# A new table of steps for the projections of two 16-wide attentions

## The chip, the cores and the metric

The program runs on one core of a Trainium2 chip. The metric is the device time of one execution in microseconds. Three runs of the kernel before took 2673.93, 2677.01 and 2681.13 us; the median is 2677.01.

## What is computed

Sixteen sequences (`B`) of 112 positions (`S`) and 256 features pass through eight layers, four attentions over a context of 375 positions and four expert layers, each with a layer norm ahead and its result added to `x`. The change touches the first and the last attention, which have 16 heads of width 16:

```python
qh = heads(layernorm(x) @ Wq + bq);  kh = heads(ctx @ Wk + bk)
vh = heads(ctx)                      # first attention
vh = heads(ctx @ Wv + bv)            # last attention; scores masked by position
att = softmax(qh @ kh.T / sqrt(16), axis=-1)
x = x + merge(att @ vh) @ Wo + bo
```

## The kernel before

Both attentions are one function, `narrow_attention_phase` (L549), called as `a0` with `ctx` (values are the context itself) and as `a6` with `Wv`, `bv` and a mask. A layer norm phase goes ahead of each; its SyncE block already fetches weights, the context of two batches and constants.

Each engine has its own program, written out in an order that is a function of a step number `s`; semaphores tie the programs together. One step is one pair of heads of one batch: step `s` holds the score product of pair `s` (`score`, L919, 112 x 375 for two heads) and the *turned* scores of pair `s - 13` (`LAG` = 13; `score_turned`, L931: context positions by queries, with the negated maximum added in the product through two more rows of keys and queries). A batch is eight steps, so what belongs to batch `b` is placed by `t = s - 8b`, and below "step 0 to 7" is `t` modulo 8. VectorE takes the maximum of every score pair (`maximum`, L850), ScalarE the exponential of every turned pair (`exponentiate`, L786). In every odd step TensorE also multiplies two pairs with the values (`weigh`, L950), the *values product*. Scores and turned scores share three double banks in rotation.

All else TensorE does are *units*, given by `units_at(s)`: they all use the one PSUM bank `p`, so each waits until the one before it has been emptied (`emptied`), TensorE waiting in order. The units, who empties the bank, and where they stand before:

- `k` (two halves of the key projection of a batch, 6 matmuls each, L970; ScalarE L809 to `raw`, then GpSimd L749 and L751 split it into high and low parts): t = -13, -12, that is steps 3, 4
- `q` (two halves of the query projection of four batches, 4 fp32 matmuls each, L974; same way): t = -11, -10 of every fourth batch, steps 5, 6
- `v` (last attention only, L981, emptied by ScalarE L815): t = 5 (12 matmuls, two thirds) and 7 (6 matmuls)
- `m` (the split maxima turned, L988; ScalarE L821, then two DMAs L716 into the query rows): t = 10, step 2
- `turn_y` (L993; emptied by VectorE's reciprocal L865 and product `yn` L867): t = 22, step 6
- `turn_n` (L996; ScalarE L823): t = 24, step 0; `out` (L999; VectorE L873 adds to `X`): t = 25, step 1
- `w` (last attention only, once, at the first step: the bias of the values through `Wo`, added by VectorE L892)

Ahead of a key projection the context is loaded by SyncE (`load_context`, L630, t = -24), copied to fp16 by ScalarE (`high_context`, L793, t = -17) and its low part made by GpSimd (`split_context`, L755, t = -16). After it SyncE copies the split keys in six DMAs to their rows (`stack_keys`, L695; two more of the mask, L700, in the last attention; t = -11); the split queries likewise (`stack_queries`, L709, t = -9 of every fourth batch); `stack_maxima` is at t = 10, and `load_values` (L633, first attention) at t = -6. GpSimd also adds the output bias to `X` (L778) and copies the values (L773). VectorE splits a batch's maxima (L856, L858) at t = 8. Within a step each engine goes through its list in a fixed order: ScalarE first `high_context`, then `exponentiate`, then the emptying of the bank; GpSimd first the splits of units, then `split_context`; SyncE goes through the batches from the lowest up, so `stack_keys` of an older batch stands ahead of `load_context` of a newer one in the same step. Nothing passes anything else on its engine. Steps begin at `FIRST` = -14.

Of the kernel before, what the change touches and what calls it, by code (L numbers as in the profile page):

```python
# [14 lines left out]
B, S, D = 16, 112, 256  # L15
SK, KT, KP = 375, 3, 125
DC = D // 128
H = 16
# [530 lines left out]
def narrow_attention_phase(nc, tag, X, XT, ident, ctxT, Wq, Wk, Wo, bo, bq, bk, ctx=None, Wv=None, bv=None, mask=None):  # L549
# [8 lines left out]
    SLOTS = ((HI, HI), (LO, HI), (HI, LO))  # L558
    N_STACK = 2 * len(SLOTS) + (2 if mask is not None else 0)
    N_CONST = 2 * (2 if mask is not None else 1)  # L560
    FIRST, LAST = -14, 8 * (B - 1) + LAG + 12

    def units_at(s):

        found = [("w", 0, 0)] if s == FIRST and bv is not None else []
        for b in range(B):
            t = s - 8 * b
            found += [("k", b, t + 13)] if t in (-13, -12) else []
            found += [("q", b // GT, t + 11)] if t in (-11, -10) and b % GT == 0 else []
            found += [("v", b, (t - 5) // 2)] if t in (5, 7) and Wv is not None else []  # L570
            found += [("m", b, 0)] if t == 10 else []
            found += [("turn_y", b, 0)] if t == LAG + 9 else []
            found += [("turn_n", b, 0)] if t == LAG + 11 else []
            found += [("out", b, 0)] if t == LAG + 12 else []
        return found

    order = [unit for s in range(FIRST, LAST + 1) for unit in units_at(s)]
# [8 lines left out]
    with ExitStack() as st:  # L586
# [98 lines left out]
        with nc.Block() as block:  # L685
            @block.sync
            def _(sp):
                def stack_keys(b):
                    u = b % 4
                    sp.wait_ge(low_made, raw_number["k", b, 1] + 1)  # L690
                    if b >= 4:
                        sp.wait_ge(shifted, NP * (b - 3))
                    for r in range(2):
                        for i, (_, part) in enumerate(SLOTS):
                            sp.dma_start(k[64 * r + 16 * i:64 * r + 16 * i + 16, u, :, :],  # L695
                                         k_parts[:, b % 2, part, r, :]).then_inc(k_in[u], 16)
                        if mask is not None:
                            if b == 0 and r == 0:
                                sp.wait_ge(mask_made, 1)
                            sp.dma_start(k[64 * r + 48:64 * r + 50, u, :, :],  # L700
                                         mask_row[b:2 * B:B, :].unsqueeze(1).to_broadcast([2, NP, SK])).then_inc(k_in[u], 16)

                def stack_queries(g):
                    sp.wait_ge(low_made, raw_number["q", g, 1] + 1)
                    if g >= 2:
                        sp.wait_ge(shifted, NP * GT * (g - 1))
                    for r in range(2):
                        for i, (part, _) in enumerate(SLOTS):
                            sp.dma_start(q[64 * r + 16 * i:64 * r + 16 * i + 16, g % 2, :, :],  # L709
                                         q_parts[:, part, r, :]).then_inc(q_in[g % 2], 16)  # L710

                def stack_maxima(b):
                    g, t = divmod(b, GT)
                    sp.wait_ge(emptied, number["m", b, 0] + 1)
                    for r in range(2):
                        sp.dma_start(q[64 * r + KS:64 * r + KM, g % 2, :, t * S:(t + 1) * S],  # L716
                                     mT[16 * r:16 * r + 16, b % 2, :]).then_inc(m_in[b % 2], 16)

                for s in steps:
                    for b in range(B):  # L720
                        t = s - 8 * b
                        if t == -11:
                            stack_keys(b)
                        if t == -9 and b % GT == 0:
                            stack_queries(b // GT)
                        if t == -6 and ctx is not None and b >= 2:
                            sp.wait_ge(v_made, b - 1)
                            load_values(sp, b)
                        if t == -24 and b >= 2:
                            sp.wait_ge(kc_split, b - 1)  # L730
                            load_context(sp, b)
                        if t == 10:
                            stack_maxima(b)

            @block.gpsimd
            def _(pool):
# [24 lines left out]
                for s in steps:  # L761
# [2 lines left out]
                            split(unit)  # L764
                    for b in range(B):
                        t = s - 8 * b
                        if t == -16 and b >= 1:
                            split_context(b)
                        if t == 8 and ctx is not None:
                            pool.wait_ge(v_in[b % 2], 16 * (b // 2 + 1))  # L770
# [10 lines left out]
            def _(act):  # L781
# [7 lines left out]
                def high_context(b):  # L789
                    act.wait_ge(kc_in[b % 2], 16 * (b // 2 + 1))  # L790
                    if b >= 4:
                        act.wait_ge(projected, number["v" if Wv is not None else "k", b - 4, 1] + 1)
                    act.copy(kc16[:, b % 4, HI, :, :], kc[:, b % 2, :, :]).then_inc(kc_hi, 1)  # L793

                def take_y(b):
# [5 lines left out]
                def evacuate(unit):  # L801
# [7 lines left out]
                        act.activation(raw[:, n % 2, 0:width], p_bank[:, 0:width], ACT.Identity,  # L809
                                       bias=bias[:, c:c + 1], scale=by).then_inc(emptied, 1)  # L810
                    elif kind == "v":
                        blocks = (2, 1)[c]
                        if b >= 2:
                            act.wait_ge(weighed, 4 * (b - 1))
                        act.mul(values[:, b % 2, 2 * c:2 * c + blocks, :, 0:HD],  # L815
                                p_bank[0:KP, 0:blocks * D].rearrange("p (j h d) -> p j h d", h=H, d=HD),
                                1.0 / WS).then_inc(emptied, 1)
                    elif kind == "m":
                        if b >= 2:
                            act.wait_ge(m_in[b % 2], 32 * (b // 2))  # L820
                        act.copy(mT[:, b % 2, :], p_bank[0:32, 0:S]).then_inc(emptied, 1)  # L821
                    else:
                        act.copy(yT[:, :, :], p_bank[:, 0:DC * S].rearrange("p (c s) -> p c s", s=S)).then_inc(emptied, 1)  # L823
# [7 lines left out]
                act.wait_ge(ones_made, 1)  # L831
                for s in steps:
                    for b in range(1, B):
                        if s == 8 * b - 17:
                            high_context(b)
                    p = s - LAG
                    if 0 <= p < NPAIR:
# [8 lines left out]
            def _(dve):  # L846
# [36 lines left out]
                for s in steps:  # L883
                    if 0 <= s < NPAIR:
                        maximum(s)
                    for b in range(B):
                        if s == 8 * b + 8:
                            split_maxima(b)
                    for kind, b, _ in units_at(s):
                        if kind == "w":  # L890
# [9 lines left out]
            def _(pe):  # L900
# [35 lines left out]
                def weigh(n):  # L936
# [4 lines left out]
                    if blk == 0:  # L941
                        if ctx is not None:
                            pe.wait_ge(v_made, b + 1)
                        else:
                            pe.wait_ge(emptied, number["v", b, 1] + 1)
                        if b >= 1:
                            pe.wait_ge(y_out, b)
                    for j in range(KT):
# [7 lines left out]
                def project(unit):  # L956
# [18 lines left out]
                                           start=i == 0, stop=i == DC - 1)  # L975
                    elif kind == "v":
                        pe.wait_ge(w_split, 2)
                        for j in ((0, 1), (2,))[c]:
                            for n, (x, z) in enumerate(PARTS):
                                for i in range(DC):  # L980
                                    mm = pe.matmul(p_bank[0:KP, (j % 2) * D:(j % 2 + 1) * D],  # L981
                                                   kc16[:, b % 4, x, i, j * KP:(j + 1) * KP], wv16[:, z, i, :],
                                                   start=n == i == 0, stop=(n, i) == (2, DC - 1))
                    elif kind == "m":
                        pe.wait_ge(split_done, b + 1)
                        if b == 0:
# [1745 lines left out]
```

## Time and profile before

| | us |
|---|---|
| median of 3 runs | 2677.01 |
| profiled execution | 2686.12 |
| its span | 2684.2 |
| TensorE busy in the span | 2262.7 (84%) |
| VectorE, ScalarE, GpSimd busy | 1483.1, 1281.2, 954.4 |

The profiled execution is one run; its span goes from the first to the last instruction, and the rest of its time lies around it. "Busy" is time in which an instruction of the engine runs. Times in the rows are microseconds from the span's start. PEclk is the granted clock of TensorE as a share of full speed (1.00 is 2.4 GHz, 0.50 is 1.2 GHz). The name behind `<-` in square brackets is what ended the idle time before an instruction. The name before `<-` in an instruction is the tile it writes, those behind it the ones it reads. A DMA's duration on SyncE is that of its issue; when its data has landed is told by the DMA view.

### The profile page before, as it was taken

What the parts mean: (1) busy time and instruction counts of PE and PEld (TensorE: products, weight loads), DVE (VectorE), ACT (ScalarE), POOL (GpSimd) and SP (SyncE); (2) the same over time, 40 slices, a digit from 0 to 9 for tenths busy, and PEclk for the clock granted to TensorE, in tenths of its full rate; (3) what the DMA queues carried; (4) which work ended last, traced back from release to release, by engine and by line L of the source; (5) the groups of instructions that cost most, each with busy time, mean ns of one, the idle gap of its engine ahead of it and who ended that gap; (6) DMA issues with size and microseconds to landing.
All of it is one profiled execution on the core that took longest, in us unless ns stands there. A gap on an engine that the chain in (4) does not pass through costs nothing. (4 is left out here: it accounts for less than half of the span.)

```text
span 2684.2 us, 60296 instructions
## 1 busy us (share of the span) xinstructions
PE 2262.7 (84%) x23000; PEld 1484.9 (55%) x23000; DVE 1483.1 (55%) x3516; ACT 1281.2 (48%) x2643; POOL 954.4 (36%) x1066
## 2 busy tenths in 40 slices
PE   4898589689999999858599999999974993899746
PEld 2555345367777777636356666666652541566523
DVE  3666482476666656456655555555555544555463
ACT  2555463265555555434355445445453542555543
POOL 3443132154445444313323233233323732333043
PEclk7898689899999999969799999999987995999868
DMA  5553271310000000010200000000023215333033
GB/s 112 107 111 81 76 235 37 106 31 14 14 14 8 14 14 2 2 32 1 90 8 13 8 13 14 8 13 8 1 79 98 68 59 121 75 76 72 19 113 109
DMA packets 118570, 139.43 MB, mean 52 GB/s; under 512 B 15072, under 2 KB 107184, under 8 KB 118288
## 3 DMA queue, kind: packets, MB, share of 16 engines
q1 hardware_dynamic: 110900, 115.39, 16.6%
q0 software_dynamic: 7392, 20.19, 2.4%
q8 instruction: 192, 3.15, 0.5%
q14 instruction: 86, 0.70, 0.1%
HBM read 93.25 MB, written 17.47 MB: 41 GB/s over the span
## 5 line engine op out<-in xcount | busy, mean ns | idle before, releaser
L850 DVE TENSOR_REDUCE a_mx<-a_pair 112x2 f32<-112x750 f32 x256 | 234.4, 934 | 203.7 <-PE a_pair L919 203.6
L302 POOL TENSOR_SCALAR a_P<-a_P,a_inv 112x375 f32<-112x375 f32 x256 | 148.4, 593 | 454.8 <-DVE a_inv L412 454.8
L1160 POOL TENSOR_TENSOR a_kp<-a_kp 125x512 f16<-125x512 f32 x192 | 217.6, 1158 | 259.2 <-ACT a_kp L1251 259.2
L786 ACT ACTIVATE a_PT<-a_pair 125x672 f32<-125x672 f32 x256 | 186.4, 731 | 101.1 <-PE a_pair L931 99.4
L340 ACT ACTIVATE a_P<-a_masked,a_least 112x375 f32<-112x375 f32 x256 | 153.5, 601 | 100.6 <-DVE a_least L407 100.6
L407 DVE CUSTOM_DVE_ANT_0 a_masked<-a_s,a_mask_add 112x375 f32<-112x375 f32 x256 | 129.6, 544 | 59.5 <-PE a_s L507 59.5
L427 DVE SCALAR_TENSOR_TENSOR a_k<-a_p,a_k 128x375 f16<-128x375 f32 x128 | 70.4, 550 | 152.9 <-ACT a_k L351 152.9
L474 PE MATMUL a_p<-a_kc,a_wk 128*128 128x375 f16 x768 | 147.0, 327 | 4.9 <-POOL a_kc L296 4.1
L1251 ACT CAST a_kp<-a_kp 125x512 f16<-125x512 f32 x192 | 110.4, 617 | 76.3 <-DVE a_kp L1313 76.3
L1393 PE MATMUL a_p<-a_kc,a_wk 128*128 128x375 f16 x768 | 142.2, 326 | 5.4 <-POOL a_kc L1152 5.4
L1294 DVE SCALAR_TENSOR_TENSOR a_k<-a_p,a_k 128x375 f16<-128x375 f32 x128 | 69.3, 547 | 139.0 <-ACT a_k L1207 138.9
L488 PE MATMUL a_p<-a_wv,a_kc 128*125 128x512 f16 x576 | 142.4, 383 | 2.6 <-DVE a_k L427 2.5
L1393 PE MATMUL a_p<-a_wv,a_kc 128*125 128x512 f16 x576 | 141.0, 385 | 0.0
L2322 PE MATMUL f_hb<-w_w1h,f_x 128*128 x588 | 136.1, 370 | 0.0
L2406 ACT ACTIVATE all_XT<-f_hb 128x512 f32<-128x512 f32 (+1 forms) x98 | 53.2, 549 | 160.1 <-PE f_hb L2322 124.2
L1313 DVE TENSOR_SCALAR a_kp<-a_p 125x512 f32<-125x512 f32 x192 | 122.7, 680 | 8.2 <-PE a_p L1424 8.2
L351 ACT ACTIVATE a_k<-a_p 128x375 f16<-128x375 f32 x128 | 61.8, 483 | 124.7 <-PE a_p L474 124.7
L517 PE MATMUL a_t<-all_ident,a_P 112*125 112x112 f32 x768 | 116.3, 287 | 0.3 <-POOL a_P L302 0.3
L419 DVE COPY a_PT<-a_t 125x336 f32<-125x336 f32 x256 | 115.4, 492 | 1.2 <-PE a_t L517 1.1
L931 PE MATMUL a_pair<-a_q,a_k 50*125 50x112 f16 (+1 forms) x1536 | 93.2, 229 | 25.6 <-DVE a_mx L850 17.5
L517 PEld LDWEIGHTS a_t<-all_ident,a_P 112*125 112x125 f32 x768 | 93.4, 188 | 36.0 <-issue 34.9
L970 PE MATMUL a_p<-a_kc,a_wk 128*128 128x375 f16 x384 | 89.5, 379 | 25.9 <-POOL a_kc L755 10.8
(415 smaller groups left out, 5170.4 us busy)
## 6 DMA issues: line engine op xcount, KB each, us to landing
a_kc<-in_ctxT SPq DMA_DIRECT2D x64, 375.0 KB, 3.6
a_k<-a_k_parts SPq DMA_DIRECT2D x192, 93.8 KB
w_stage<-in_L_ffn_W SPq DMA_DIRECT2D x32, 512.0 KB
w_stage<-in_L_ffn_ew SPq DMA_DIRECT2D x16, 512.0 KB, 7.0
w_stage<-expert_rows SPq DMA_DIRECT2D x16, 448.0 KB, 7.5
a_v_in_sb<-in_ctx SPq DMA_DIRECT2D x16, 375.0 KB
a_q<-a_q_parts SPq DMA_DIRECT2D x48, 112.0 KB, 3.6
w_stage<-in_L_ffn_W SPq DMA_DIRECT2D x16, 256.0 KB, 4.0
```

The costliest lines, as they stand in the source:

```text
L302: pool.tensor_scalar(P[:, p % 4, r, :], P[:, p % 4, r, :], inv[:, p % 4, r:r + 1], 1.0, ALU.mult, ALU.mult).then_inc(P_done, 1)
L340: act.activation(P[:, p % 4, r, :], masked[:, p % 2, r, :], ACT.Exp, bias=least[:, p % 4, r:r + 1], scale=-1.0, accum_out=total[:, p % 4, ...
L407: dve.tensor_tensor_reduce(masked[:, p % 2, r, :], s_bank[0:S, r, 0:SK], mask_add[:, b % 2, :], 1.0, 3e38, ALU.add, ALU.min, least[:, p % ...
L474: mm = pe.matmul(out[:, 0:SK], wk16[:, z, j, c * 128:(c + 1) * 128], kc16[:, b % 2, x, j, :], start=i == j == 0, stop=(i, j) == (2, DC - 1))
L488: mm = pe.matmul(out[0:KP, 0:512], kc16[:, b % 2, x, j, jk * KP:(jk + 1) * KP], wv16[:, z, j, w * 512:(w + 1) * 512], start=i == j == 0, s ...
L517: mm = pe.transpose(t_bank[0:KP, r, j * S:(j + 1) * S], P[:, p % 4, r, j * KP:(j + 1) * KP], ident[0:S, 0:S])
L786: act.activation(PT[:, p % 4, :, :], pair_bank[slot["turned", p]][0:KP, :, 0:KT * S], ACT.Exp).then_inc(exp_done, 1)
L850: dve.tensor_reduce(mx[:, b % 2, 2 * pair:2 * pair + 2], pair_bank[slot["score", p]][0:S, :, 0:SK], AX.X, ALU.max).then_inc(max_done, 1)
L1160: pool.tensor_tensor(kp16[:, LO, j, hf, r, :, :].rearrange("p c m -> p (c m)"), kp[:, n % 4, :], kp16[:, HI, j, hf, r, :, :].rearrange("p ...
L1313: dve.tensor_scalar(kp[:, n % 4, :], p_bank[bank][0:KP, 0:512], 0.0, EPS * WS, ALU.max, ALU.add).then_inc(f_evac, 1)
L1393: mm = pe.matmul(out, lhs(x, z, j), rhs(x, z, j), start=i == j == 0, stop=(i, j) == (2, DC - 1))
L2322: mm = pe.matmul(bank[:, 0:BW], x16[:, j % 2, x, c, :], w.w1h[:, z, c, bass.ds(e, 1), cols].rearrange("p o f -> p (o f)"), start=False, st ...
```

## The change

`units_at` reads its places from named constants, some of which are new:

- `k` at t = -16 and -12 (steps 0 and 4) instead of -13 and -12
- `q` at t = -29 and -21 of every fourth batch (both step 3, eight steps apart) instead of -11 and -10; stack_queries at -13 instead of -9
- `v` as three units of 6 matmuls at t = 5, 6, 7 instead of two of 12 and 6
- `m` at t = 9 instead of 10, VectorE's split of the maxima at 7 instead of 8
- `turn_n` at t = 25 instead of 24, `out` at 26 instead of 25
- `load_context` at t = -27 instead of -24, `high_context` at -21 instead of -17, `split_context` at -19 instead of -16
- steps begin at -29, so the first group's order is q, q, k, k instead of k, k, q, q; the last step is one later

Where two units fall in one step, the one of the older batch goes first: `turn_n` ahead of `m` in step 1, `turn_y` ahead of `v` in step 6. The amounts of work are unchanged.

```diff
--- before.py
+++ after.py
@@ -558,20 +558,22 @@
     SLOTS = ((HI, HI), (LO, HI), (HI, LO))
     N_STACK = 2 * len(SLOTS) + (2 if mask is not None else 0)
     N_CONST = 2 * (2 if mask is not None else 1)
-    FIRST, LAST = -14, 8 * (B - 1) + LAG + 12
+    FIRST, LAST = -29, 8 * (B - 1) + LAG + 13
+    K_AT, Q_AT, V_AT, M_AT = (-16, -12), (-29, -21), (5, 6, 7), 9
+    TURN_Y, TURN_N, OUT = LAG + 9, LAG + 12, LAG + 13
 
     def units_at(s):
 
         found = [("w", 0, 0)] if s == FIRST and bv is not None else []
         for b in range(B):
             t = s - 8 * b
-            found += [("k", b, t + 13)] if t in (-13, -12) else []
-            found += [("q", b // GT, t + 11)] if t in (-11, -10) and b % GT == 0 else []
-            found += [("v", b, (t - 5) // 2)] if t in (5, 7) and Wv is not None else []
-            found += [("m", b, 0)] if t == 10 else []
-            found += [("turn_y", b, 0)] if t == LAG + 9 else []
-            found += [("turn_n", b, 0)] if t == LAG + 11 else []
-            found += [("out", b, 0)] if t == LAG + 12 else []
+            found += [("k", b, K_AT.index(t))] if t in K_AT else []
+            found += [("q", b // GT, Q_AT.index(t))] if t in Q_AT and b % GT == 0 else []
+            found += [("v", b, V_AT.index(t))] if t in V_AT and Wv is not None else []
+            found += [("m", b, 0)] if t == M_AT else []
+            found += [("turn_y", b, 0)] if t == TURN_Y else []
+            found += [("turn_n", b, 0)] if t == TURN_N else []
+            found += [("out", b, 0)] if t == OUT else []
         return found
 
     order = [unit for s in range(FIRST, LAST + 1) for unit in units_at(s)]
@@ -721,12 +723,12 @@
                         t = s - 8 * b
                         if t == -11:
                             stack_keys(b)
-                        if t == -9 and b % GT == 0:
+                        if t == -13 and b % GT == 0:
                             stack_queries(b // GT)
                         if t == -6 and ctx is not None and b >= 2:
                             sp.wait_ge(v_made, b - 1)
                             load_values(sp, b)
-                        if t == -24 and b >= 2:
+                        if t == -27 and b >= 2:
                             sp.wait_ge(kc_split, b - 1)
                             load_context(sp, b)
                         if t == 10:
@@ -764,7 +766,7 @@
                             split(unit)
                     for b in range(B):
                         t = s - 8 * b
-                        if t == -16 and b >= 1:
+                        if t == -19 and b >= 1:
                             split_context(b)
                         if t == 8 and ctx is not None:
                             pool.wait_ge(v_in[b % 2], 16 * (b // 2 + 1))
@@ -789,7 +791,7 @@
                 def high_context(b):
                     act.wait_ge(kc_in[b % 2], 16 * (b // 2 + 1))
                     if b >= 4:
-                        act.wait_ge(projected, number["v" if Wv is not None else "k", b - 4, 1] + 1)
+                        act.wait_ge(projected, number[("v", b - 4, 2) if Wv is not None else ("k", b - 4, 1)] + 1)
                     act.copy(kc16[:, b % 4, HI, :, :], kc[:, b % 2, :, :]).then_inc(kc_hi, 1)
 
                 def take_y(b):
@@ -809,11 +811,9 @@
                         act.activation(raw[:, n % 2, 0:width], p_bank[:, 0:width], ACT.Identity,
                                        bias=bias[:, c:c + 1], scale=by).then_inc(emptied, 1)
                     elif kind == "v":
-                        blocks = (2, 1)[c]
                         if b >= 2:
                             act.wait_ge(weighed, 4 * (b - 1))
-                        act.mul(values[:, b % 2, 2 * c:2 * c + blocks, :, 0:HD],
-                                p_bank[0:KP, 0:blocks * D].rearrange("p (j h d) -> p j h d", h=H, d=HD),
+                        act.mul(values[:, b % 2, c, :, 0:HD], p_bank[0:KP, 0:D].rearrange("p (h d) -> p h d", d=HD),
                                 1.0 / WS).then_inc(emptied, 1)
                     elif kind == "m":
                         if b >= 2:
@@ -831,7 +831,7 @@
                 act.wait_ge(ones_made, 1)
                 for s in steps:
                     for b in range(1, B):
-                        if s == 8 * b - 17:
+                        if s == 8 * b - 21:
                             high_context(b)
                     p = s - LAG
                     if 0 <= p < NPAIR:
@@ -884,7 +884,7 @@
                     if 0 <= s < NPAIR:
                         maximum(s)
                     for b in range(B):
-                        if s == 8 * b + 8:
+                        if s == 8 * b + 7:
                             split_maxima(b)
                     for kind, b, _ in units_at(s):
                         if kind == "w":
@@ -942,7 +942,7 @@
                         if ctx is not None:
                             pe.wait_ge(v_made, b + 1)
                         else:
-                            pe.wait_ge(emptied, number["v", b, 1] + 1)
+                            pe.wait_ge(emptied, number["v", b, 2] + 1)
                         if b >= 1:
                             pe.wait_ge(y_out, b)
                     for j in range(KT):
@@ -975,12 +975,10 @@
                                            start=i == 0, stop=i == DC - 1)
                     elif kind == "v":
                         pe.wait_ge(w_split, 2)
-                        for j in ((0, 1), (2,))[c]:
-                            for n, (x, z) in enumerate(PARTS):
-                                for i in range(DC):
-                                    mm = pe.matmul(p_bank[0:KP, (j % 2) * D:(j % 2 + 1) * D],
-                                                   kc16[:, b % 4, x, i, j * KP:(j + 1) * KP], wv16[:, z, i, :],
-                                                   start=n == i == 0, stop=(n, i) == (2, DC - 1))
+                        for n, (x, z) in enumerate(PARTS):
+                            for i in range(DC):
+                                mm = pe.matmul(p_bank[0:KP, 0:D], kc16[:, b % 4, x, i, c * KP:(c + 1) * KP], wv16[:, z, i, :],
+                                               start=n == i == 0, stop=(n, i) == (2, DC - 1))
                     elif kind == "m":
                         pe.wait_ge(split_done, b + 1)
                         if b == 0:
```

## Rows read from the trace of the kernel before

**Rows 1.** Windows: stretch, length, busy time (instructions) by engine, clock, DMA share, GB/s
```profile
51.65:108.42 56.77, 46.04 (x468) 24.80 (x469) 33.86 (x43) 25.40 (x41) 26.35 (x33) 0.76 0.57 103
108.42:246.60 138.18, 124.57 (x1850) 78.30 (x1846) 90.43 (x131) 83.45 (x144) 64.03 (x79) 0.99 0.53 107
164.34:176.89 12.55, 11.58 (x187) 7.51 (x183) 8.54 (x14) 8.15 (x15) 5.81 (x8) 1.00 0.53 109
2273.32:2333.80 60.48, 52.34 (x541) 31.48 (x541) 32.38 (x43) 28.91 (x48) 24.02 (x29) 0.84 0.39 84
2333.80:2491.95 158.15, 145.34 (x2029) 97.19 (x2028) 87.54 (x130) 93.55 (x163) 57.44 (x71) 1.00 0.32 71
2398.30:2413.03 14.73, 13.76 (x202) 9.44 (x201) 8.50 (x13) 9.15 (x16) 5.06 (x7) 1.00 0.25 67
```

**Rows 2.** Timeline, TensorE, plain batch, first attention: start, duration (us), line, shapes, [idle <-releaser]
```profile
166.09 0.78 PE L950 MATMUL a_y<-a_PT,a_values 125*32 125x112 f32 x24
166.80 1.12 PE L999 MATMUL a_p<-a_wo,a_yT 128*112 128x256 f32 x4
167.85 0.37 PE L919 MATMUL a_pair<-a_k,a_q 48*112 48x375 f16 x2
...
170.31 1.14 PE L970 MATMUL a_p<-a_kc,a_wk 128*128 128x375 f16 x6
...
171.37 0.37 PE L919 MATMUL a_pair<-a_k,a_q 48*112 48x375 f16 x2
...
172.11 1.14 PE L970 MATMUL a_p<-a_kc,a_wk 128*128 128x375 f16 x6 [0.20 <-ACT a_raw L809]
```

**Rows 3.** Timeline, TensorE, second query product of a pair, first attention
```profile
147.49 1.77 PE L974 MATMUL a_p<-all_XT,a_wq 128*128 128x448 f32 x4 [0.81 <-DVE a_yn L867]
```

**Rows 4.** Timelines of ScalarE, GpSimd, SyncE; DMA view (us to landing) of two loads
```profile
173.28 0.57 ACT L809 ACTIVATE a_raw<-a_p,a_bkT 128x375 f32<-128x375 f32 x1 [0.60 <-PE a_p L970]
...
173.76 0.73 ACT L786 ACTIVATE a_PT<-a_pair 125x672 f32<-125x672 f32 x1
...
175.63 0.81 ACT L793 CAST a_kc<-a_kc 128x750 f16<-128x750 f32 x1
...
173.92 0.50 POOL L749 CAST a_k_parts<-a_raw 128x375 f16<-128x375 f32 x1 [0.26 <-ACT a_raw L809]
174.50 0.90 POOL L751 TENSOR_TENSOR a_k_parts<-a_raw,a_k_parts 128x375 f16<-128x375 f32 x1
...
162.87 3.80 SPq L695 DMA_DIRECT2D a_k<-a_k_parts  x6
...
a_kc<-in_ctxT SPq DMA_DIRECT2D x1, 375.0 KB, 4.1
...
a_kc<-in_ctxT SPq DMA_DIRECT2D x1, 375.0 KB, 5.2
```

**Rows 5.** Timeline, TensorE, values projections of a batch, last attention
```profile
2408.27 1.52 PE L981 MATMUL a_p<-a_wv,a_kc 128*125 128x256 f16 x12
...
2412.23 0.87 PE L981 MATMUL a_p<-a_wv,a_kc 128*125 128x256 f16 x6
```

**Rows 6.** Timelines of TensorE and ScalarE, starts of both attentions
```profile
34.33 3.36 PE L974 MATMUL a_p<-all_XT,a_wq 128*128 128x448 f32 x4 [0.66 <-ACT a_raw L809]
...
52.48 0.82 ACT L793 CAST a_kc<-a_kc 128x750 f16<-128x750 f32 x1 [1.70 <-DMA a_kc<-in_ctxT]
...
2273.32 1.19 PE L919 MATMUL a_pair<-a_k,a_q 50*112 50x375 f16 x6 [1.94 <-DMA a_q<-a_q_parts]
...
2276.77 2.04 PE L970 MATMUL a_p<-a_kc,a_wk 128*128 128x375 f16 x6 [1.30 <-POOL a_kc L755]
```

**Rows 7.** Timelines of VectorE (two splits of maxima) and GpSimd, first attention
```profile
151.83 2.82 DVE L858 SCALAR_TENSOR_TENSOR a_m<-a_mx,a_m 112x16 f16<-112x16 f32 x1
...
165.93 0.18 DVE L858 SCALAR_TENSOR_TENSOR a_m<-a_mx,a_m 112x16 f16<-112x16 f32 x1
...
153.11 1.51 POOL L755 TENSOR_TENSOR a_kc<-a_kc 128x750 f16<-128x750 f32 x1
```

## Prediction

> **What bounds the kernel now.** The change touches one function, which runs twice: the first attention (scores start at 51.65 us) and the last one (2273.32). I first measured, with the windows view, the stretch from one score product to another. A batch of 112 queries is eight steps, one pair of heads each. In the middle of the first attention a batch without a query projection takes 12.55 us, in which TensorE is busy for 11.58, VectorE for 8.54, ScalarE for 8.15 and GpSimd for 5.81, at full clock (1.00, the 2.4 GHz level); in the last attention it is 14.73, with TensorE at 13.76 [rows 1]. So TensorE's own sequence sets the step, and what can be won is only its holes. Ten batches in the middle take 138.18 and 158.15 us; ten plain ones would be 125.5 and 147.3, so each of the two pairs of query projections among them costs (138.18 - 125.5) / 2 = 6.3 and 5.4 us. The first four batches take 56.77 and 60.48 us, at a mean clock of 0.76 and 0.84: there the 1.2 GHz level and the hand-overs count.
>
> The holes are read in the TensorE timeline. A values product (weigh) and what stands before the next unit takes 166.80 - 166.09 = 0.71 us; the output product 1.05; a key projection 171.37 - 170.31 = 1.06, the second of the pair starting 0.2 late because the single bank `p` is still being emptied by ScalarE [rows 2]. A score and its turned scores take 0.47 without a wait (estimate from the same starts). Plain sum: 8 x 0.47 + 4 x 0.71, the two key products, output 1.05, turns and maxima about 1.3: some 11.1, so 1.4 of 12.55 us is waiting: mostly a turned score behind VectorE's maximum after a step shorter than 1.2 us, the early second key product, and the y copy. For queries: 1.77 us each at full clock, and the second waits 0.81 more for `a_yn`, since it follows turn_y in one step [rows 3].
>
> **The change, part by part (first attention, plain batch).** I walk the new order through with these durations, step 0 starting at 0. Step 0: turned score still behind the last maximum of the batch before (0.54), then key product 0: 1.9. Step 1: score, turned, values product 1.18, turn_n 0.34, then the maxima's product, which now stands right behind turn_n in the same bank and waits for ScalarE's copy (0.5 estimate): 2.2. Step 2 gets the output product: 1.55. Step 3 loses its key product: 1.18. Step 4: 1.6, its wait on the bank gone. Steps 5, 6, 7 as before: 1.18, 1.45, 1.18. Sum 12.26, so at most 0.3 us a batch. Splitting maxima one step sooner costs VectorE the same two short operations; the maxima's DMAs start as much sooner as the steps between got shorter, and are needed 2.8 us later, as now.
>
> The queries stand alone in step 3 of two different batches: 1.77 plus 0.25 because step 4's key product then waits for the bank: 2.0 each, 4.0 a pair.
>
> **The moved context.** high_context goes from t=-17 to -21 and its load from -24 to -27. But SyncE issues in order, and at t=-27 the load stands behind stack_keys of an older batch, which waits for GpSimd's split of a key product of the step before; so far it was sent right behind these too. The load thus leaves no sooner, while ScalarE wants it four steps sooner, in front of an exp. That closes a ring: copy 0.81, two exps 2 x 0.73, evacuation 0.57, GpSimd 0.50 + 0.90, six key issues 3.80, landing 4.1 (5.2 at another batch) [rows 4]; with some 0.4 for hand-overs 12.5 us, or 13.6 with the later landing. It is as long as the batch. I take 12.65 for a batch without a query product, near the shorter landing, to which most are close. A batch with one has room: 12.26 + 2.0 = 14.3. The batch after the queries' stacking has 6 more DMAs ahead of keys and context: its context lands later by an estimated 1.3 us, near the 1.1 between the two landings (bounds 0 and 2.2). Four batches: 14.3 + 14.3 + 12.35 (room from before) + 13.6 = 54.5; ten: 2 x 54.5 + 2 x 12.65 = 134.3 against 138.18: **-3.9** (ring never binding, no backlog: 10 x 12.26 + 8.0 = 130.6, -7.6; ring at 13.6: 4 x 14.3 + 6 x 13.6 = 138.8, +0.6).
>
> **The last attention** has no load of values (ring shorter than the batch) but values projections. Now 12 matmuls in step 5 (1.52 us as drawn) and 6 in step 7 (0.87) [rows 5], each 0.07 less to the next start, as the key product in [rows 2]; after, 6 in each of steps 5, 6, 7: 2.4, that is +0.15. The one in step 6 stands behind turn_y in the same bank, and waits for the reciprocal and `yn` on VectorE, as the second query product does now (0.81) [rows 3]. In exchange the short steps are filled, and waits behind maxima go, 0.7. Walked through as above: 1.62 + 2.18 + 1.52 + 1.18 + 1.63 + 1.98 + 2.91 + 1.98 = 15.0, +0.3. Ten batches: 150.0 + 2 x 4.0 = 158.0 against 158.15: **-0.2** (no wait in step 6: -4; half a microsecond more a batch: +3). The two last batches add 0.3 each: **+0.5**, with the last units one step later at no cost, as no product is left in between.
>
> **The starts** are where I expect the loss. Query products come first: 3.36 us each at half clock [rows 6]. In the first attention they can start 3 us before the first key product could, so, by these durations in a row, the first score comes at about 47.7 instead of 51.65 (this time and those that follow are estimates of the same kind). But then: SyncE loads context 2 only behind stack_keys(0) (about 44.7, landing at 49); ScalarE at s=-5 waits for it *before* it evacuates the second key product of batch 1 (s=-4); GpSimd splits that one (1.4) and only then the context (1.6); and the key product that needs it stands at s=0 right behind the first score. It starts at about 53.5, and TensorE idles for 5 us. Then come the query product for the next group (3.36 + 0.6) and its evacuation behind the wait for context 3 (1.4). Score 8 is then at +3.8, score 16 at +6.1 (+4.9 if the clock has risen, +7.3 if not), and the 6.3 of the query pair is gone from batches 2 and 3: **-0.2** (-2.9 to +1.8).
> In the last attention the head start doesn't exist: the bias product `w` holds the bank until VectorE has added it, so queries start where keys did. First score +1.7 (eight key DMAs now come last); key product of batch 2 at 2280.2 instead of 2276.77 [rows 6], another +1.8; query product at half clock +4.0; ScalarE's wait for context 3 +1.8; one hand-over more among the values units +0.6: +9.9 at score 8. The other query product adds 2.5 (0.7 at full clock, 4.3 at half), and 5.4 comes back in batch 2: **+7.0** (+5.2 to +10).
>
> **Sum.** -0.2 - 3.9 + 7.0 - 0.2 + 0.5 = **+3.2 us**. The profiled execution took 2686.12 us (span 2684.2 and 1.9 around it), 9.1 above the median 2677.01 of three runs; the difference applies to both: 2689.3 profiled, **2680** as a median. A measurement of this kernel can tell about 0.3%, 8 us, from no change.
>
> **VectorE against GpSimd.** In a batch after a query pair a maxima split (L858) takes 2.82 us and ends with GpSimd's context split, which began after it and took 1.51; the same operation takes 0.18 where it isn't met [rows 7]. It delays the maxima behind it by 2.6 us. In the new order the context split (step 5) ends about 0.7 us before the maxima split begins, and the key split comes 2 us after it; that gain is in the 6.3 above.
> The Trainium skill (SBUF — State Buffer, "Who interferes with whom") says that a VectorE instruction with two SBUF inputs contends with a GpSimd instruction that reads SBUF, and that the first takes the shared pair for a whole instruction while the other fully blocks. The row doesn't agree in size: the wait of 2.6 is longer than any one GpSimd instruction there. The sum stays by either, as it is taken from the measured 138.18; the collision rival below would cost 1.2 us a batch by the rule and 2.3 by the row.
>
> **Rivals.**
> - *Slower: the context ring and chain.* For it: one landing of 5.2 us, the copy already waiting on it at the first batches [rows 4, 6], and a load that does not leave sooner. Against: most landings near 4.1. It decides from a landing of about 4.6 us on. Price: middle +0.6 instead of -3.9, first start +3.8, last start +10, the rest +0.3: +14.7, **2692**.
> - *Faster: the clock.* The starts miss 24% of full clock over 57 us and 16% over 60: 13.6 + 9.7 = 23 us where TensorE is the bound [rows 1]. If the longer unbroken stretches of query products win half of that back, the starts give +6.8 - 11.7 = -4.9, and all together -4.9 - 3.9 - 0.2 + 0.5 = -8.5: **2668**. Against: the 5 us hole in front of batch 2's keys.
> - *The split still collides.* If the later context copy makes GpSimd late by over 0.7 us, L858 blocks until that one instruction ends (1.5), in every batch, and with it step 1's turned score, which has 0.3 to spare: 1.2 x 10 on top of 3.2: +15, **2692**.
> - *The moved units do nothing for the middle*, because each wait comes back at another hand-over (ring at 12.55): +3, inside the forecast.
>
> **Chances.** Forecast (with the last rival) 0.47, faster by the clock 0.25, ring 0.19, collision 0.09. Faster by over 0.3%: 0.26; within: 0.47; slower: 0.27. Of the forecast's own bounds, 2672 to 2688. Range over the cases: **2665 to 2692**.
>
> **What would show it.** Plain batches of the first attention at 12.3 to 12.8 us, with ScalarE's idle time before the context copy released by the DMA; query pairs at 4 instead of 6.3; L858 at 0.18 everywhere; in the last attention, 15.0 a batch, with the second values unit waiting on `a_yn`; TensorE idle for about 5 us after the first scores, then waiting on `a_kc` from GpSimd. The prediction is wrong if score 32 of the last attention doesn't come later than 60.48 us after its first, if the context copy never waits on its DMA, or if the clock in the starts rises above 0.9.

## The result and the profile after

The changed kernel is **slower by 0.46%**: 2688.58 us median (2684.38 to 2694.59, 11 runs) against 2676.66 (2669.36 to 2681.13, 11 runs), ratio 1.0046 with a 95% interval of 1.0038 to 1.0054: +12 us, where +3 was forecast. It lies within the range (2665 to 2692), just above the forecast's own bounds (2672 to 2688), and in the class "slower by over 0.3%", which had a chance of 0.27. The first lines of its page:

```profile
span 2686.7 us, 60342 instructions
PE 2241.7 (83%) x23000; PEld 1480.5 (55%) x23000; DVE 1477.8 (55%) x3516; ACT 1294.0 (48%) x2659; POOL 956.6 (36%) x1066
```

The spans differ by 2.5 us only. That agreement with the sum is chance: the last expert layer, in which no line differs, takes 138.42 us in the profile before and 124.53 in this one (last section). The answer to [rows 1] is the windows view of the same stretches, from score 0 to score 32 and on to score 112, in both attentions, with single batches between them:

```profile
48.54:116.60 68.06, 46.74 (x467) 25.98 (x467) 32.24 (x45) 26.43 (x42) 27.08 (x32) 0.70 0.51 90
116.60:264.15 147.55, 125.39 (x1852) 81.81 (x1848) 86.42 (x129) 85.86 (x143) 63.99 (x80) 0.93 0.54 98
207.30:219.44 12.14, 11.32 (x188) 7.53 (x185) 8.69 (x14) 8.29 (x15) 5.71 (x8) 1.00 0.82 138
219.44:240.14 20.70, 13.23 (x189) 8.89 (x185) 8.96 (x14) 8.40 (x15) 5.91 (x8) 0.84 0.59 93
2288.39:2353.80 65.41, 52.08 (x539) 32.50 (x539) 32.52 (x45) 30.89 (x53) 24.77 (x29) 0.83 0.41 78
2353.80:2510.37 156.57, 142.60 (x2027) 96.81 (x2026) 87.84 (x130) 99.02 (x173) 57.53 (x71) 1.00 0.35 72
2402.28:2417.17 14.89, 13.60 (x203) 9.41 (x201) 8.78 (x13) 9.67 (x17) 5.05 (x6) 1.00 0.41 64
```

Its columns are those of [rows 1]. Third and fourth line are two neighbouring batches of the first attention, 10 and 11. A plain one now takes 12.14 (12.55 before), and the next 20.70, with the same work. Batches 3, 7 and 11 take 21.98, 20.84 and 20.69; the others of the middle 11.9 to 15.3. These are the batches that follow the stacking of a group's queries. ScalarE's waits in 116.60 to 264.15 (us in all, times, longest):

```profile
ACT a_kc L795 <- DMA a_kc<-in_ctxT: 24.4, 7, 8.4
ACT a_PT L788 <- PE a_pair L931: 19.6, 35, 1.3
```

The longest of the first kind, in the timeline (start, duration, and in brackets the idle time ahead of it), and the issue of the load that it waits for:

```profile
221.88 0.59 SPq L632 DMA_DIRECT2D a_kc<-in_ctxT  x1
...
233.29 0.82 ACT L795 CAST a_kc<-a_kc 128x750 f16<-128x750 f32 x1 [8.44 <-DMA a_kc<-in_ctxT]
```

The load was issued at 221.88, behind six key DMAs, which stand behind six query DMAs and a values load. It landed some 11.3 us later (an estimate: the copy that waits for it starts 11.4 after the issue), not 4.1 to 5.2 as in [rows 4]. TensorE stops, and afterwards the granted clock is 0.56, near the 1.2 GHz level, where 1.00 stood before. The windows view of batch 11:

```profile
221.50:225.50 4.00, 3.56 (x55) 2.47 (x53) 2.22 (x3) 2.49 (x5) 2.85 (x4) 1.00 1.15 123
225.50:227.30 1.80, 1.80 (x40) 1.23 (x37) 1.59 (x3) 0.00 (x0) 0.00 (x0) 1.00 0.91 146
227.30:233.30 6.00, 0.63 (x4) 0.18 (x2) 0.28 (x1) 0.01 (x1) 0.00 (x0) 0.93 0.35 84
233.30:240.14 6.84, 5.35 (x78) 4.00 (x78) 3.18 (x5) 5.01 (x8) 2.98 (x3) 0.56 0.22 63
```

In the six dead microseconds the DMA engines are at a mean share of 0.35 and 84 GB/s, though work is waiting. That would fit a last part of the backlog that lies on some of the engines only; the view doesn't name them, so this isn't shown.

### The profile page after: what moved, and what is told of

It is laid out like the page before. It is cut to its first block and busy times, and to the rows that moved or that the text cites. A ratio compares the mean times of both kernels' runs of the same rounds, so it can differ in the third digit from the quotient of the medians.

```text
span 2686.7 us, 60342 instructions
## 1 busy us (share of the span) xinstructions
PE 2241.7 (83%) x23000; PEld 1480.5 (55%) x23000; DVE 1477.8 (55%) x3516; ACT 1294.0 (48%) x2659; POOL 956.6 (36%) x1066
## 5 line engine op out<-in xcount | busy, mean ns | idle before, releaser
L340 ACT ACTIVATE a_P<-a_masked,a_least 112x375 f32<-112x375 f32 x256 | 153.5, 601 | 100.7 <-DVE a_least L407 100.7
L919 PE MATMUL a_pair<-a_k,a_q 48*112 48x375 f16 (+1 forms) x512 | 98.1, 386 | 28.0 <-ACT a_PT L788 21.5
```

The source lines that it names most:

```text
L340: act.activation(P[:, p % 4, r, :], masked[:, p % 2, r, :], ACT.Exp, bias=least[:, p % 4, r:r + 1], scale=-1.0, accum_out=total[:, p % 4, ...
```

## The experiments

Each job timed the kernel before on the same chip; its median was 2676.6 for e1 to e4 and 2689.5 to 2689.8 for e5 to e12, so only ratios are compared. The letters in the expectations are explanations: A (and A'), the query DMAs delay the context; B, the loss is in the last attention; C, the context copy stands too early; E, stacking and values load together ask more of the DMA engines than a batch allows; F, a stall follows every stacking.

**Which attention.** e1 has the new table in the first attention only, e2 in the last only. They choose it by a flag, `NEW = Wv is None` in one and `Wv is not None` in the other:

```diff
-    FIRST, LAST = -29, 8 * (B - 1) + LAG + 13
+    FIRST, LAST = (-29, 8 * (B - 1) + LAG + 13) if NEW else (-14, 8 * (B - 1) + LAG + 12)
...
+    STACK_Q, LOAD, COPY, SPLIT, MAXIMA = (-13, -27, -21, -19, 7) if NEW else (-9, -24, -17, -16, 8)
```

> The new table in the first attention only, the old one in the last. Theory A (the loss is the query stacking DMAs of t=-13, which hold up the context in the first attention, three times): the full kernel was 12 us above before; the first attention's phase grew by 12 us in the profiles, the last one's by 3. So about +9 to +12 us against before, with the 8 us steps at step 4 of batches 3, 7 and 11. Rival B (the loss sits in the last attention's start and values units): +2 us or less.

> The new table in the last attention only. Theory A: +1 to +4 us against before: start +6, middle -1.6, an end that is shorter. Rival B: +9 or more.

e1: 1.0058 (1.0041 to 1.0075), that is +15.5 us; e2: 1.0004 (0.9995 to 1.0013). So the loss is in the first attention; in the last one it is at most the +3.5 us of the interval's end. The profiles of the same job say it too: from the first attention's layer norm to the next phase 304.90 in e1 and 288.54 in e4 (the kernel before), and the last attention's phase 318.90 in e2 and 319.30 in e4. My main loss, the last attention's start, does not show in the time. By attention the forecast was -4.1 and +7.3 us, and the runs have +15.5 and +1.1.

**Queries stacked later.**

```diff
-                        if t == -13 and b % GT == 0:
+                        if t == -9 and b % GT == 0:
```

> The changed kernel with one number back: the queries are stacked at t=-9 (step 7, after the keys and the context load of step 5 have been issued) instead of -13 (step 3, right behind the values load). Theory A: the waits of ScalarE's context copy on its DMA fall from 8 us to about 1, step 4 of batches 3, 7, 11 from 8 to 9 us to about 1.7, the three batches from 21 to 13 or 14 us: 20 us less than the changed kernel, about 8 us below before. Rival C (the context copy at t=-21 is too early whatever stands in the queue; the ring of 12.5 us binds): less than 8 us is won back and the batches stay above 16 us.

1.0044 (1.0027 to 1.0060): nothing won, the expectation missed. The middle of the first attention is 140.88 instead of 147.55, but the last attention's rises to 162.35. Batch 7 still takes 18.23. TensorE now waits for the maxima, whose DMAs stand behind the queries, and ScalarE still for the context. From the waits views of ScalarE and of TensorE, 107 to 249 us:

```profile
ACT a_kc L795 <- DMA a_kc<-in_ctxT: 13.8, 7, 3.7
PE a_pair L931 <- DMA a_q<-a_mT: 7.4, 3, 3.0
```

**The kernel before again.**

> The kernel before, unchanged, for a second profile. The profiled execution shown was 9 us above the median of its runs, and its last phase (the last expert layer, 138.4 us) is 13.9 us longer than in the changed kernel, where no line of it differs. If that was chance of one execution, this profile has it at 124 to 130 us and a span near 2675; if the changed kernel really shortens it, it is 138 again.

Its last expert layer took 123.69 us: the 138.42 shown before is not the old kernel's. Its other stretches repeat [rows 1] within 0.3, but for the last attention's start, 63.55 instead of 60.48, and that phase as a whole, 319.30 instead of 312.76.

**The context copied later.**

```diff
-                        if s == 8 * b - 21:
+                        if s == 8 * b - 18:
...
-                        if t == -19 and b >= 1:
+                        if t == -17 and b >= 1:
```

> The changed kernel with the context copy at t=-18 (step 6) and its low part at -17 (step 7) instead of -21 and -19; loads and all else as changed. Theory C (the early copy turns late landings into stalls, whatever delays them): the load that now takes 11.3 us to land, because six query DMAs, a values load and six key DMAs are ahead of it, is wanted 4.6 us later, so ScalarE's wait of 8.4 us falls to some 4; batches 3, 7, 11 of the first attention go from 21 to about 16.5 us: 13 us less than the changed kernel. Both starts gain 2 to 3 us each, since the copy for batch 2 no longer stands ahead of batch 1's second key product: 2669 to 2674. Rival A (only the amount of DMA ahead matters): no more than 4 us less than the changed kernel.

1.0007 (0.9996 to 1.0019): by the ratios 10 us less than the changed kernel, but not where expected. The ten middle batches, where 13 us were to be won, give 3.3 (144.21 against 147.55). The copy waits for no DMA any more in the middle, yet batches 7 and 11 still take 17.52 and 20.82: the stall moved to the next thing that the same queue delivers. From TensorE's waits, 48.56 to 254.82:

```profile
PE a_pair L931 <- DMA a_q<-a_mT: 18.5, 3, 7.9
```

The starts did gain, 6 us in the first attention (68.06 to 62.05) and 7 in the last (65.41 to 58.35). The last attention's start takes 64.9 to 65.6 us in six profiles with the new table and the early copy (the changed kernel and e2, e6, e8, e9, e10), and 56.8 to 58.5 in the four with the late copy (e5, e7, e11, e12). The windows view of e5, the first attention's ten batches and the last one's start:

```profile
110.61:254.82 144.21, 125.38 (x1850) 81.60 (x1846) 86.33 (x129) 86.33 (x143) 64.33 (x80) 0.94 0.52 97
2276.15:2334.50 58.35, 48.19 (x539) 30.05 (x540) 32.50 (x45) 30.32 (x52) 23.57 (x27) 0.90 0.47 85
```

So theory C (the early copy makes the stall) falls for the middle, with the queue in this order, and holds for the starts.

**The burst in halves**, alone and with the late copy:

```diff
-                    for r in range(2):
+                    for r in sides:
...
-                            stack_queries(b // GT)
+                            stack_queries(b // GT, (0, 1) if b == 0 else (0,))
+                        if t == -5 and b % GT == 0 and b > 0:
+                            stack_queries(b // GT, (1,))
```

> The changed kernel with the burst of query DMAs parted: three of six at t=-13, the other three eight steps later at t=-5 (first group as before). Theory A' (the burst of DMAs ahead of keys and context is what makes the load late): landing falls from 11.3 to about 7 us, the waits of the copy from 8.4 to 3 or 4, now in two batches of four; the sum over a group falls by 3 to 6 us, 9 to 15 us less in all than the changed kernel. Theory C alone: 5 us less or nothing, as the wait is only spread.

> Both edits together. If early copy and burst are the two factors, no wait of the copy on its DMA is left in the middle batches: 12.2 us plain, 13.7 to 14 with a query product, four batches 52 to 53 us where the changed kernel has 69 and the kernel before 56 to 57; middle of the first attention 130 to 132 us against 147.5; the starts as in the kernel with the late copy. 2658 to 2666 in all, clearly below the kernel before.

1.0037 (1.0021 to 1.0054) and 1.0024 (1.0012 to 1.0035). Halves bring batches 7 and 11 from 21 to 18.8; three query DMAs suffice for a stall here. Together with the late copy it is worse than the late copy alone, a clear miss: the second half comes too late for the scores (waits of 11.2 us in three), and the maxima are late too (11.6 in three).

**What the backlog is made of.** The values load moved (`t == -2` instead of -6), left out, and the stackings of groups 2 and 3 left out. In e9 and e10 the waits that counted on what is gone are shortened to match; both leave out work that the result needs, so they serve for reading the traces alone:

```diff
-                        if t == -6 and ctx is not None and b >= 2:
+                        if False:
...
-                        if t == -13 and b % GT == 0:
+                        if t == -13 and b % GT == 0 and (ctx is None or b < 2 * GT):
```

> The changed kernel with the values load of the first attention at t=-2 (step 6, after keys and context of step 5) instead of -6 (step 2, just ahead of the queries). If the 375 KB of the values are a full part of the backlog: landing of the context after a query stacking 8 to 9 us instead of 11.3, batches 3, 7, 11 at 18 to 19 us instead of 21. If only the query DMAs count, they stay at 20 to 22.

> The changed kernel without the loads of the values of batches 2 to 15 in the first attention (the values of batches 0 and 1 are used again, so that part of the result is left out). Theory E (in the first attention the batch that holds the stacking of queries asks more of the DMA engines than its 12.2 us allow; in the last attention, which has no values load and 14.9 us a batch, the same stacking causes no wait): without 375 KB a batch, batches 3, 7, 11 fall from 21 to 12.5 to 14 us. If the six query DMAs alone did it, they stay above 18.

> The changed kernel without the query stacking of groups 2 and 3 in the first attention (the projections are still made and split; the old rows are used, so the scores of batches 8 to 15 are not the reference's). Theory E and theory A alike: batches 7 and 11 fall from 21 to 12.2 us, batch 3 stays at 21 to 23; the landing of the context there is 4 to 5 us. If they stay long, the queries' DMAs are not what delays the context.

e8: batches 3, 7, 11 fall to 12.93, 12.73, 12.14, and the batches ahead of them rise to 18.41, 20.13, 20.17, TensorE waiting for maxima (14.0 us in three): moved again. e9: batch 7 takes 14.37 and batch 11 13.44. e10: 12.96 and 13.05, while batch 3, whose stacking was left in, stays at 22.04. The ten batches and batch 7 of e9, in the windows view:

```profile
107.42:240.56 133.14, 121.21 (x1850) 78.93 (x1847) 87.03 (x131) 85.38 (x144) 64.09 (x81) 0.99 0.46 82
147.91:162.28 14.37, 12.52 (x188) 8.27 (x185) 9.53 (x16) 8.31 (x15) 5.91 (x8) 0.91 0.41 82
```

The same of e10:

```profile
114.37:246.78 132.41, 121.07 (x1850) 78.52 (x1846) 86.21 (x129) 85.17 (x143) 63.89 (x80) 0.99 0.48 99
155.52:168.48 12.96, 11.38 (x188) 7.57 (x184) 8.69 (x14) 8.18 (x15) 5.71 (x8) 1.00 0.56 107
```

Either load alone costs 0.8 to 2.2 us above a plain batch; both together, in this order and in a batch of 12 us, cost 8.6 to 9.8. That the stall needs both is shown by taking away each of them. That the length of the batch matters is argued: in the last attention the same six query DMAs, without a values load and in 14.9 us a batch, cause no such stall (14.89 for batch 7), but there both differ.

**The query products put beside the stacking.** The late copy is in both attentions. In the first one the query products also move, and the queries are stacked after the keys and the context load:

```diff
+    if Wv is None:
+        FIRST, Q_AT, STACK_Q, COPY, SPLIT = -19, (-13, -9), -8, -18, -17
```

> As the kernel with the late copy in both attentions, and in the first one the two query products are put into the batch whose stacking follows (t=-13 and -9, steps 3 and 7 of batches 2, 6, 10), stacked at t=-8. Theory E (the DMA engines need some 30 us for the two batches around a stacking, whatever TensorE does, so the products should be spent there): batches 2 and 3 of a group stay at 30 to 31 us together, batches 0 and 1 fall from 13.9 to 12.15: a group 54.5 to 55.5 us where the changed kernel has 61 to 62 and the kernel before 55.9 to 57.2; against the kernel before 8 to 12 us less. Rival F (a stall of 6 to 8 us follows a stacking, whatever is beside it): a group stays at 58 to 61 us.

0.9983 (0.9972 to 0.9994): 4 us under the kernel before, not 8 to 12. Batches 0 and 1 of a group fall to 12.14, but the two around the stacking take 15.77 and 18.25, 34.0 and not 30: a group 58.3, which is what rival F asked for. It isn't rival F's stall, though. From score 32 to score 112 no engine waits for a DMA. What holds up batch 7 is read in the timelines of TensorE, GpSimd and SyncE:

```profile
153.56 1.12 PE L977 MATMUL a_p<-a_kc,a_wk 128*128 128x375 f16 x6 [3.56 <-POOL a_kc L762]
...
150.27 0.56 POOL L756 CAST a_q_parts<-a_raw 128x448 f16<-128x448 f32 x1 [4.24 <-ACT a_raw L816]
150.91 1.03 POOL L758 TENSOR_TENSOR a_q_parts<-a_raw,a_q_parts 128x448 f16<-128x448 f32 x1
151.90 1.51 POOL L762 TENSOR_TENSOR a_kc<-a_kc 128x750 f16<-128x750 f32 x1
...
151.97 3.77 SPq L716 DMA_DIRECT2D a_q<-a_q_parts  x6
```

TensorE wants the low part of the context in step 0. GpSimd makes it only behind the split of the second query product, which e12 put into step 7, just ahead of it. The wait begins before the first query DMA is issued, and it stands in all three such batches (10.7 us together). The rest of the 6 us is the clock, 0.81 over the batch. So e12 shows a new wait on GpSimd, and no stall of the queue at all. Whether 30 us would be enough for the DMA engines (theory E) stays open, and a context split ahead of the query split was not tried.

**A version that beats both.**

> The old table in the first attention; the new one in the last, with the context copy at t=-18 and its low part at -17 there. The phase of the last attention was 308 us with this copy, 315 to 319 with the changed kernel's and 313 to 319 before: so 5 to 9 us below the kernel before, the only version so far that is faster than both. If the gain of the copy lies in the first attention alone, no difference from the kernel before.

The old table in the first attention, the new one with the late copy in the last: **0.9968 (0.9957 to 0.9979)**, 8 us under the kernel before, the lowest of all versions; e12 is the only other one below it. Its windows (first attention's ten batches, last one's start and ten batches) are the old ones in the first attention and e5's in the last:

```profile
106.68:245.34 138.66, 124.69 (x1852) 78.52 (x1848) 90.70 (x131) 83.43 (x144) 64.08 (x79) 0.99 0.54 106
2267.82:2326.35 58.53, 48.28 (x539) 30.16 (x540) 32.53 (x45) 30.28 (x52) 23.54 (x27) 0.90 0.47 85
2326.35:2482.92 156.57, 142.59 (x2027) 96.81 (x2026) 87.84 (x130) 98.02 (x173) 57.80 (x71) 1.00 0.36 72
```

## Why the prediction was right, and where it was not

The time lies in the range and on the side that was forecast, but this is luck in part. The forecast put the whole loss into the last attention and a gain into the first; e1 and e2 show it the other way round. The walk through the steps and the starts' mechanism held, one step failed badly, and an error of the other sign hid part of it. By stretches of the profiles (starts counted from the layer norm's first instruction, 11.13 and 2233.04 before, 11.27 and 2246.61 after), in us:

| term | forecast | measured |
|---|---|---|
| first attention, to score 32 | -0.2 | +8.0 |
| first attention, ten batches | -3.9 | +9.4 |
| last attention, to score 32 | +7.0 | +6.4 |
| last attention, ten batches | -0.2 | -1.6 |
| last batches and ends, both | +0.5 | -7.3 |
| both phases | +3.2 | +14.9 |

The rest of the span gave -12.4, of it -13.9 in the last expert layer; with +14.9 that is the 2.5 between the spans. Single profiles are a weak measure of two of the terms:

- The last attention to score 32, counted like this, took 100.7 and 106.2 us in the two profiles of the kernel before and 102.1 in e1, which has the old table there, so its +6.4 may be as little as +1.0. The changed kernel's last attention phase (315.53) is 2.8 longer than that of the profile before (312.76) and 3.8 shorter than e4's.
- The -7.3 of the ends is for the most part the clock of this one execution. From score 112 of the first attention to the next phase the changed kernel took 48.34 us at a mean granted clock of 0.91; e1 and e10, with the same table there, took 55.61 at 0.71; the kernel before 53.60 at 0.76. The windows view, changed kernel and then e1:

```profile
264.14:312.48 48.34, 36.16 (x619) 24.36 (x615) 20.49 (x36) 25.34 (x43) 3.67 (x5) 0.91 0.08 22
260.67:316.28 55.61, 45.05 (x619) 30.33 (x615) 20.76 (x38) 25.53 (x43) 3.67 (x5) 0.71 0.07 19
```

What held and what failed:

- **The failed step** is "its context lands later by an estimated 1.3 us (bounds 0 and 2.2)". The batch after a stacking took 20.7 to 22.0 us, 8.6 to 9.8 above the plain 12.14, three times: 27 us where I had some 4. The load landed 7 us later than in a plain batch, not 1.3. I took the bound from the spread of two landings that stood in no such queue. What I should have asked is what is issued ahead of the context load within one batch, before and after, and how soon the copy wants it. In the kernel before, too, the load stood right behind the six query DMAs, but the values load came after it, the keys had gone out 4 us earlier, and the copy asked for it only at 163.07 (L793) and didn't wait:

```profile
144.61 3.80 SPq L695 DMA_DIRECT2D a_k<-a_k_parts  x6
151.70 3.90 SPq L709 DMA_DIRECT2D a_q<-a_q_parts  x6
155.65 0.60 SPq L630 DMA_DIRECT2D a_kc<-in_ctxT  x1
156.85 1.35 SPq L716 DMA_DIRECT2D a_q<-a_mT  x2
158.25 0.42 SPq L633 DMA_DIRECT2D a_v_in_sb<-in_ctx  x1
```

- **The ring of 12.5 to 13.6 us** did not bind: plain batches took 12.14, where the sum had 12.65 and the walk 12.26, though the copy's short waits on the DMA (1.1 to 2.2 us) are there. Its danger was named in the right place and priced wrong, as a steady half microsecond and not as a stall of 8 us. The measured time is nearer to this rival's 2692 than to the forecast's 2680, but not by its mechanism.
- **The walk through the steps held.** Plain batches 12.14 (12.26 forecast) and 14.89 (15.0); a query pair in the last attention 3.9 (16.82 twice against 14.89) where 4.0 was forecast; the values unit behind turn_y waits 0.8 for `a_yn`.
- **The starts held in their mechanism**, though for the last attention e2's time doesn't show the loss: first score at 48.54 (47.7), the key product of batch 2 at 53.92 (53.5), after a hole of 4.81 that GpSimd's split ends:

```profile
53.92 2.04 PE L970 MATMUL a_p<-a_kc,a_wk 128*128 128x375 f16 x6 [4.81 <-POOL a_kc L757]
```

  The +8.0 of the first attention's start is the stall of batch 3; with a plain 12.14 there the start would be at -1.8. That the early copy costs 6 to 7 us in the starts is shown by e5, and by e11 in the last attention. The upper bound of +10 for the last start doesn't follow from its own terms (9.9 + 4.3 - 5.4 = 8.8).
- **VectorE against GpSimd**: L858 takes at most 176 ns in the whole changed kernel, so [rows 7] are gone, as said; the collision rival did not come. The 2.82 us of the kernel before lie beside three GpSimd instructions back to back (151.63 to 154.62 us), so the rule of the Trainium skill (SBUF — State Buffer, "Who interferes with whom") may have acted once for each; no run here measures a single collision.
- The clock rival fell: 0.70 and 0.83 in the starts, where 0.76 and 0.84 stood.

## What to carry to other kernels

When the order of transfers or the length of a batch changes, write down what is issued ahead of each load in one period, and when its reader wants it. Six query DMAs and a values load, both ahead of the keys and the context load, cost 8.6 to 9.8 us in a batch of 12.1; in the kernel before, with the values load behind and a later copy, the batch after the stacking was 1.4 us above a plain one (13.97 against 12.55).

A stall that moves from one waiting instruction to another when one of them is relaxed (context copy, maxima, scores, in e3, e5, e7 and e8) belongs to what they share, here the queue. But name the wait anew each time: the 18.25 us of e12 look like the same stall and are a wait for GpSimd.

A sum that fits the profile is not confirmed while phases outside the change differ, or while a term that fits does so by the clock of one execution.

## What the runs showed of the hardware

- The last expert layer took 122.9 to 127.7 us in five profiles (the changed kernel and e1 to e4 among them) and 136.4 to 141.9 in nine others, those of e5 to e12 and the first one of the kernel before; its code and TensorE time are much the same. In e1 to e12 the two kinds go with the jobs, not with the kernels, and so does the median of the kernel before (2676.6 with the short kind, 2689.5 to 2689.8 with the long one); why is open. The windows view of that layer in the changed kernel:

```profile
2562.14:2686.67 124.53, 67.42 (x505) 41.45 (x505) 74.67 (x243) 50.00 (x119) 54.32 (x55) 0.73 0.41 124
```

And in e11:

```profile
2534.70:2672.90 138.20, 70.67 (x505) 41.71 (x505) 74.93 (x243) 49.34 (x119) 53.90 (x55) 0.73 0.39 111
```

- A context load of 375 KB landed 4.2 us after its issue in plain batches and 11.3 after a stacking, with a mean DMA share of 0.35 in the last 6 us. Why the share is so low while a load is waited for is open; another queue for the queries was not tried.
- In the end of the first attention the same instructions took 48.3 us at a mean granted clock of 0.91 and 55.6 at 0.71 in different executions (the changed kernel, e1).
